# Five of eight wo products taken from the first phase of a layer kernel and made in the passage to attention

## The reference

```
x = x + mamba_and_ffn(L(x))      # state-space mixer with a scan over tokens, then a ReLU FFN 256 -> 1024 -> 256
x = x + gated(L(x))              # first use of the gated block
x = x + attention(L(x))          # 16 heads of 16
x = x + gated(L(x))              # second use, same weights

def gated(x):                    # the leading axis (8 sequences) is the step of a recurrence
    def step(c, xt):
        ft = sigmoid(xt @ wf.T + c @ uf.T + bf)
        it = sigmoid(xt @ wi.T + c @ ui.T + bi)
        gt = tanh(xt @ wc.T + c @ uc.T + bc)
        c = ft * c + it * gt
        return (c, None)
    c_final, _ = lax.scan(step, c0, x)
    return tanh(einsum('tbi,oi->tbo', x, wo) + c_final @ uo.T + bo)
```

## Time and profile before

| | us |
|---|---|
| median of 3 runs | 1632.35 |
| lowest and highest | 1628.58, 1634.82 |
| the profiled execution's own time | 1629.72 |
| its span, first to last instruction | 1627.9 |

### The profile page before, as it was taken

The page is one execution under the profiler, slowest core; times in us unless marked ns, Lnnn a source line. Parts: engine busy times, 40 slices in busy tenths (PEclk is TensorE's granted clock), DMA queues, the critical chain, the costliest instruction groups (busy, mean ns, idle before and its releaser), DMA issues.

```text
span 1627.9 us, 17393 instructions
## 1 busy us (share of the span) xinstructions
PE 1398.9 (86%) x5576; PEld 671.8 (41%) x5576; DVE 1181.1 (73%) x1836; ACT 884.7 (54%) x1513; POOL 684.1 (42%) x400
## 2 busy tenths in 40 slices
PE   6534889999999998999957999999999999989994
PEld 2202344545353545465432333434444443434442
DVE  3698898989898998860168777676868677666225
ACT  5564858585857664622212565546565655555533
POOL 2577878787879777621314122212130212100000
PEclk9866899999999999999976999999999999999997
DMA  6515161606161515100255333333232432320044
GB/s 199 174 42 192 40 221 39 222 28 221 40 207 54 193 54 181 52 26 17 62 136 117 72 80 81 91 69 77 55 91 67 92 79 50 83 53 15 15 156 142
DMA packets 93787, 158.05 MB, mean 97 GB/s; under 512 B 8592, under 2 KB 74704, under 8 KB 90576
## 3 DMA queue, kind: packets, MB, share of 16 engines
q1 hardware_dynamic: 93696, 156.94, 33.5%
HBM read 110.91 MB, written 46.01 MB: 96 GB/s over the span
## 4 chain that ended last, share of the span: by engine, by line
PE 62%; DVE 20%; issue 10%; ACT 4%; POOL 2%; DMA 2%; SPq 0%; DVEq 0%; POOLq 0%; ACTq 0%
PE psum L990 24%; PE psum L1945 8%; PE psum L1879 7%; PE psum L1853 7%; PE psum L1824 6%; PE psum L1868 5%; DVE psum L543 5%; DVE mx L1347 4%; PE psum L1035 2%; DVE middle L505 2%; DVE hb L543 1%; DVE hb L546 1%; PE psum L1819 1%; DVE stats L1323 1%; DVE bg_stats L473 1%
## 5 line engine op out<-in xcount | busy, mean ns | idle before, releaser
L1347 DVE TENSOR_REDUCE mx<-psum 128x1 f32<-128x512 f32 x512 | 344.5, 686 | 186.1 <-PE psum L1853 183.0
L1604 ACT ACTIVATE pw<-psum 128x512 f32<-128x512 f32 x512 | 301.7, 598 | 301.7 <-PE psum L1868 299.0
L920 POOL TENSOR_TENSOR hb<-ddb,bcb 128x1024 f32<-128x1024 f32 x128 | 309.7, 2442 | 65.5 <-DVE middle L505 51.6
L543 DVE TENSOR_TENSOR_SCAN psum<-psum,hb 128x512 f32<-128x512 f32 x224 | 261.5, 1213 | 29.6 <-ACT psum L736 18.1
L1853 PE MATMUL psum<-kp,qp 96*128 96x512 bf16 x512 | 208.6, 409 | 37.7 <-DVE mx L1347 27.8
L736 ACT ACTIVATE psum<-ddb,A_neg 128x512 f32<-128x512 f32 x256 | 165.3, 681 | 79.7 <-DVE hb L546 60.2
L1868 PE MATMUL psum<-qp,kp 99*128 99x512 bf16 x512 | 199.0, 390 | 8.2 <-ACT pw L1604 6.5
L1762 POOL TENSOR_TENSOR rstd<-rstd,neg_half 128x4 f32<-128x4 f32 x16 | 16.3, 1018 | 446.5 <-DVE rstd L1332 446.5
L546 DVE TENSOR_TENSOR hb<-psum,bcb 128x1024 f32<-128x1024 f32 x112 | 137.2, 1225 | 3.9
L1879 PE MATMUL psum<-pw,v_sb 128*32 128x512 f32 x1024 | 134.7, 647 | 0.5 <-ACT pw L1604 0.5
L990 PE MATMUL psum<-back,w 128*128 128x512 f32 x256 | 115.3, 605 | 8.3 <-ACT back L752 8.3
(11 more groups left out here) (200 smaller groups left out, 2203.7 us busy)
## 6 DMA issues: line engine op xcount, KB each, us to landing
ddb<-dd SPq DMA_DIRECT2D x64, 512.0 KB, 6.1
bcb<-bc SPq DMA_DIRECT2D x32, 512.0 KB, 6.5
parts<-parts_sb SPq DMA_DIRECT2D x96, 128.0 KB
dd<-dd_out SPq DMA_DIRECT2D x8, 1024.0 KB, 4.8
qp<-parts SPq DMA_DIRECT2D x32, 256.0 KB, 8.0
kp<-parts SPq DMA_DIRECT2D x16, 384.0 KB, 4.5
x_front<-x_dram SPq DMA_DIRECT2D x8, 512.0 KB, 4.0
xh<-x_front SPq DMA_DIRECT2D x8, 512.0 KB, 4.5
```

The source lines that it names most:

```text
L543: e.tensor_tensor_scan(to[:, g, :], a[:, g, :], h[:, g, :], 0.0, ALU.mult, ALU.add).then_inc(scan_ok, 1)
L920: e.tensor_tensor(hb[n % NHB], ddb[k % NSLOT][:, 1:2, :].to_broadcast([P, 2, L]), bcb[q][:, 0, :, :], ALU.mult).then_inc(bx_ok, 1)
L1347: used.up(e.tensor_reduce(mx[u % 2][:, n:n + 1], bank(used.n % 2), AXIS.X, ALU.max))
L1604: e.activation(pw[n % NPW], bank(5 + n % 2), ACT.Exp, scale=HD ** -0.5).then_inc(exp_ok, 1)
```

## The change

- `LATE = range(2, 7)`: for these five batches (gate parts of iterations 4 to 8) the first phase makes no xwo. SP stores the turned gate input X0 to `x_turned` instead of G2 to `xwo_first`, once ACT has copied it, and ACT's next write to X0 waits for this store.
- In the ring order, on PE and on ACT, z stands ahead of gi: ACT does z and its tanh at u = 4 and the input gate at u = 5. This holds for every iteration with both parts, 2 to 6.
- At the start of the second phase SP waits for the stores of `x_after_mamba` and `x_turned`, loads the five turned inputs (512 KB each) to `late_x`, and only then issues the first loads of x and xwo.
- PE makes the five products in ten pieces k of two tiles each, in banks 5, 6 and 7 by turns: k = 0, 1 behind the last xwo, k = 2 to 5 at p = -2, s = 13, and k = 6 to 9 one tile at each step s = 23 to 30 of p = -2. ACT copies each piece to one of three `late_out` buffers, which SP stores to `xwo_first`: three behind the second fetch, two at the end of p = -1.
- `late_x` and `late_out` lie where pw and ot of the second phase lie, and the first uses of these wait for the late stores.

```diff
         if gate:
             use("act", "gturn", i - 2, 2)
-            if i <= NB:
+            if i - 2 < LATE[0]:
                 use("act", "xwo", i - 2, 2)
-            use("act", "gi", i - 2, 2)
         if mid:
             use("act", "z", i + 1, 2)
+        if gate:
+            use("act", "gi", i - 2, 2)
...
-                if gate and i <= NB:
+                if gate and i - 2 < LATE[0]:
                     ring_out(e, "xwo", i - 2, 1)
                     e.dma_start(rows_of(xwo1_dram[i - 2]), tok(G2)).then_inc(xwo1_sent[(i - 2) % 2], 16)
+                if gate and i - 2 in LATE:
+                    ring_out(e, "gturn", i - 2, 1)
+                    e.dma_start(xT_dram[i - 2 - LATE[0]], feat(X0)).then_inc(xT_sent, 16)
...
             def gate_turned(b):
+                if b > LATE[0]:
+                    e.wait_ge(xT_sent, 16 * (b - LATE[0]))
...
-                    if u == 4 and gate:
-                        gate_i(i - 2)
-                    if u == 5 and mid:
+                    if u == 4 and mid:
                         mid_z(i + 1)
                         mid_tz(i + 1)
+                    if u == 5 and gate:
+                        gate_i(i - 2)
...
+            for i in range(2):
+                e.wait_ge(x1_sent[i], 16 * NB // 2)
+            e.wait_ge(xT_sent, 16 * len(LATE))
+            for n in range(len(LATE)):
+                if n == len(LATE) - 1:
+                    e.wait_ge(xr_ok, NB)
+                e.dma_start(late_x[n], xT_dram[n]).then_inc(late_in, 16)
             x_load(0)
...
+            for n in range(3):
+                late_store(n)
...
+                if p == -1:
+                    late_store(3)
+                    late_store(4)
...
+            def late_done(k):
+
+                n, u = divmod(k, 2)
+                e.wait_ge(late_pe, k + 1)
+                if n >= 3:
+                    e.wait_ge(late_sent[n - 3], 16)
+                e.activation(late_out[n % 3][:, 2 * u:2 * u + 2, :], halves(bank(5 + k % 3)), ACT.Copy).then_inc(late_act, 1)
...
+            def late_tile(k, t):
+
+                n, u = divmod(k, 2)
+                if t == 0:
+                    if k == 0:
+                        ring_out(e, "xwo", NB - 1, 1)
+                        e.wait_ge(late_in, 16 * len(LATE))
+                    if k >= 3:
+                        e.wait_ge(late_act, k - 2)
...
+                    if s == 13 and p == -2:
+                        for k in range(2, 6):
+                            late_tile(k, 0)
+                            late_tile(k, 1)
+                    if 23 <= s < 31 and p == -2:
+                        late_tile(6 + (s - 23) // 2, (s - 23) % 2)
```

More of the change, by code:

```diff
@@ L47 @@
 NSC = HU * NT
+LATE = range(2, NB - 1)
 class Count:
@@ L248, in build @@
         first.close()
+        between = ExitStack()
+        late_x = [place(between, f"late_x{i}", NF, L) for i in range(len(LATE))]
+        late_out = [place(between, f"late_out{i}", NT, D) for i in range(3)]
+        between.close()
         second = ExitStack()
@@ L293, in build @@
         x1_sent, xwo1_sent = [sem(f"x1_sent{i}") for i in range(2)], [sem(f"xwo1_sent{i}") for i in range(2)]
+        xT_sent, late_in, late_pe, late_act = sem("xT_sent"), sem("late_in"), sem("late_pe"), sem("late_act")
+        late_sent = [sem(f"late_sent{i}") for i in range(len(LATE))]
         f_var, f_rstd, h_raw, h_ok, xn_ok, xh_ok, sq_ok, m_ok = (sem(n) for n in (
@@ L757, in back_relu @@
                 ring_done(e, name, b, k)
-                if c == 6 and b > 0:
+                if c == 6 and 0 < b <= LATE[0]:
                     e.wait_ge(xwo1_sent[(b - 1) % 2], 16 * ((b - 1) // 2 + 1))
@@ L807, in act_first @@
                         gate_turned(i - 2)
-                    if u == 2 and gate and i <= NB:
+                    if u == 2 and gate and i - 2 < LATE[0]:
                         gate_xwo(i - 2)
@@ L1114, in pe_first @@
                     gate_turn(i - 2)
-                    if i <= NB:
+                    if i - 2 < LATE[0]:
                         gate_xwo(i - 2)
+                if mid:
+                    mid_in(i + 1, "z", 1)
+                if gate:
                     if i <= NB:
@@ L1368, in values_out @@
                 e.wait_ge(pv_pe, 8 * u + 4 * q + 4)
+                if q == 0 and u < 2:
+                    for n in range(len(LATE)):
+                        if n % 3 == u + 1:
+                            e.wait_ge(late_sent[n], 16)
                 if u >= 2 and q == 0:
@@ L1603, in weigh @@
                     e.wait_ge(pv_pe, (n - NPW) // 4 + 1)
+                if n == 2 * len(LATE):
+                    for k in range(0, len(LATE), 3):
+                        e.wait_ge(late_sent[k], 16)
                 e.activation(pw[n % NPW], bank(5 + n % 2), ACT.Exp, scale=HD ** -0.5).then_inc(exp_ok, 1)
@@ L1703, in act_second @@
                         cast(b + 2, 0, 0, s - 18)
+                    if s == 13 and p == -2:
+                        for k in range(2, 6):
+                            late_done(k)
                     if s == 19 and not odd and front and b + 2 > 0:
                         front_tanh(b + 2)
+                    if s in (25, 27, 29, 31) and p == -2:
+                        late_done(6 + (s - 25) // 2)
                     if s == 19 and p == -4:
@@ L1839, in pe_second @@
             token_product(ring("xwo", NB - 1, 1), 1, feat(X0), wo).then_inc(r_pe, 1)
+            def late_tile(k, t):
[6 more added lines that the diff above has]
+                        e.wait_ge(late_act, k - 2)
+                tile = slice((2 * u + t) * P, (2 * u + t + 1) * P)
+                ins = product(halves(bank(5 + k % 3))[:, t, :], [(late_x[n][:, j, tile], wo[:, j, :]) for j in range(NF)])
+                if t == 1:
+                    ins.then_inc(late_pe, 1)
+            for k in range(2):
+                late_tile(k, 0)
+                late_tile(k, 1)
             e.wait_ge(set_k, 3)
@@ L1866, in shifted @@
                 else:
-                    ring_out(e, "xwo", NB - 1, 1)
+                    e.wait_ge(late_act, 2 * len(LATE))
                 e.matmul(bank(5 + n % 2), kp[u % 3][0:NROW + 3, h, kt * P:(kt + 1) * P], qp[u % 3][0:NROW + 3, h, :],
```

19 lines of the change are left out of this document (14 added, 5 removed).

## The result

The kernel with the change takes 1635.92 us (median of 15 runs, 1632.46 to 1641.36), the kernel before beside it 1629.83 us (15 runs). The ratio is 1.0042, 95% interval 1.0031 to 1.0053: about 7 us slower, inside the forecast range of 1630 to 1656 and within the 0.5% that I called no change. The profiled execution took 1640.07 us (span 1638.3), 10.4 more than the profiled one of before, where I forecast 11.

The account below looks back on a forecast made before the run. PE runs gapless from the FFN to the forget gate, but DVE and ACT set the FFN's start in middle iterations. +11.7 - 3.5 + 2.8 = +11 on the median of 1632.35 gives 1643.3 us, range 1630 to 1656.

Parts of the forecast that it names:

- Part 1: Iterations 4 to 8 without xwo: 0 in iterations 4 to 7, -3.5 us in iteration 8.
- Part 2: z before gi, iterations 2 to 6: iterations 3 to 6 cost 2.5 us each, iteration 2 1.7, together +11.7.
- The idle piece: PE before gi's second half: some 8 us idle in iterations 4 to 6, 3.6 us in iterations 2 and 3.
- the clock loss: Low granted clock on PE's work behind the longer idle time, taken as 1.8 us per iteration.
- 0.7 for extra work behind the gate: PE has 1.72 us more work after its release at gi's second half, less 1.00 slack: 0.7 us per iteration.
- Iteration 7: No mid part; PE already waits 3.08 us for L752 before the FFN, so leaving out xwo gives 0.
- unchanged there: Expected sign: distance between FFN starts about 2.5 us longer until iteration 7, and unchanged at iteration 7.
- Part 3: Stores and waits of the first phase, with the late loads at its end: each 0.
- Part 4: Late product in the passage: -1.7 at the attention turn, +4.5 between scores 8 to 15, net +2.8 us.
- the wait for the late store: Passage, ACT's late copies wait for the first late store, meeting PE's last tile: 0 to +2 us.
- Rival A: Low clock stays away or is already paid: +2.8 to +5 first phase, 0 to +3 passage, 1632 to 1637; chance 0.22.

Follow-up runs that it names:

- e2: Kernel before with z ahead of gi in the ring, on PE and on ACT, no product moved: 1637.66 us, ratio 1.0052.
- e13: Kernel before with only batch 6's wo product moved to the passage, z ahead of gi, 3 dummy products between gi's halves: 1623.74 us, ratio 0.9966.
- e8: The change with dummy products between gi's halves, 3 in iterations 2 and 3, 8 in iterations 4 to 6: 1626.98 us, ratio 0.9979.
- e6: Kernel before with only batch 6's wo product (iteration 8's xwo) moved to the passage, gi ahead of z: 1628.88 us, ratio 0.9987.
- e3: The change with dummy products between gi's halves, 6 in iterations 2 and 3, 16 in iterations 4 to 6: 1649.86 us, ratio 1.0122.
- e9: Kernel before with four dummy matmuls behind the last xwo, ahead of the attention turn: 1630.74 us, ratio 1.0004.
- e5: The change with all ten late pieces ahead of the first score and five late_out buffers: 1634.56 us, ratio 1.0028.
- e1: The change with gi ahead of z again in the ring, on PE and on ACT: 1630.38 us, ratio 1.0006.

## Why the prediction was right, and where it was not

- **Part 1, xwo free in iterations 4 to 7, -3.5 in iteration 8: held.** e2 beside after and e13 beside e8 give 0 for iterations 4 to 6, e6 gives 3.44 for iteration 8. In iteration 7 the product is free too, but taking it out costs 0.36 (see iteration 7). In the profile of after iteration 8 gained 6.1: the other 2.7 are clock, which I had not forecast. The out product gives 1.7 (3.72 for 5.41), and goes either way behind the same wait of 2.27 us. The FFN that opens this column gives 1.0 (14.67 for 15.70). By the rule of the Trainium skill (Perfetto Trace Analysis, Identifying the Most-Contended Engine), read over the whole kernel, iteration 8 would have been free as well; the 3.44 us of e6 go against it.
- **Part 2, gi's second half behind z's first, at the low clock: the mechanism held, one size did not.** The idle piece was 7.90 us (forecast some 8), the clock loss 1.6 to 3.1 at gi (forecast 1.8). The 0.7 for extra work behind the gate did not show: e8 takes 84.30, before 84.34. DVE's shorter update (2.02 for 2.62, in e8 as in after) gives 0.6 of it back. And in iteration 6 I had not seen that the kernel before loses 1.5 itself (its out product takes 5.41 there), so the step is 0.5, not 2.5. Iterations 3 to 6 measured +6.8 for my +10. Iteration 2 measured +1.84 for my +1.7, counted from the start of its xwo (24.21 for 22.37), behind the scatter of the start.
- **Iteration 7, forecast 0: wrong, +1.25.** The failed step is "unchanged there", in two terms that I had put at nothing.
  - 0.89 is the out product's clock: 6.61 us for 5.72 behind the same wait of 6.57 us. In both kernels the chain that ended last runs through this product. e3 settles it against gi's new place in ACT's order: it has the input gate at u = 5 as well, its out product took 5.28, and its column reads 79.82, less than before. e2 (+1.0) is longer by this alone (6.76), e8 (+1.1) by this (6.43) and the next term. The length repeats with the code (5.72, 5.81 and 5.83 in before, e9 and e6; 6.61 in after and e5), so it goes with the code and not with the single execution; what sets it behind the same wait stays open.
  - 0.36 comes from the order and the missing xwo together. I had followed gi's move only where z stands ahead of it, but `gate_i` goes to u = 5 in iteration 7 too. Without xwo PE waits 2.94 us for it and the sums run at the low clock (3.64 us), so they and not ACT set the FFN's start. With xwo (e2, e13) the wait is 1.12, the sums take 1.92, and the 0.36 is absent.
- **Part 3, stores and loads 0:** nothing waits for them in the first phase's rows; e1's total agrees.
- **Part 4, the passage, +2.8: measured +2.69**, with its halves as worked out (first score 1.9 us earlier for my 1.7, from there to `nm` +4.6 for my +4.5). From the first of the eight tiles to score 15 it took 11.8 us for my 10.9, 0.7 of it the wait for the late store that I had put at 0 to 2. e5 shows the loss in the total. e9 shows that the gain at the turn alone would have been given back; in the change I cannot tell the two apart.
- **Behind `nm`, not forecast: +2.1 in the profile.** Kernels with late tiles read 751.3 to 753.6 there, those without 750.9 to 751.6. What costs this 1 us or so stays open; no run takes it apart.
- **The total.** The misses (-3.2 in iterations 3 to 6, -2.6 in iteration 8, +1.25, +2.1, and about +2 at the start, 1.8 of it scatter) cancel to within 1 us of the forecast in this one profile. That is partly luck: the profiled execution lies near the upper end of the 15 runs, and by the medians the step is 6 to 7, where I said 11. My 1643.3 also stood on a median of three runs, 1632.35, which over 15 is 1629.83. Rival A's range (1632 to 1637) held the median as well, for another reason than the one I gave: the low clock did come.

## What to carry to other kernels

When an engine has slack in a stretch, taking work from it there buys nothing, and leaving it idle can cost: price the longer idle piece by the clock of what comes behind it. Where a gap can't be closed, fill it with dummy work to its measured size and no further, and measure the size of one dummy first. Judge a stretch by its own start and end marks across several kernels, and then take out of it what one clock-dependent product adds: a column can grow by the clock of a product whose work and wait are the same as before. A total mixes a real effect with clock luck elsewhere, and a gain of clock at one place can be a loss at the next.

## What I had not expected of the hardware

- The same wait can be followed by either clock: behind 2.27 us ahead of iteration 8's out product the 16 passes took 5.41 us in before and e6, and 3.72 in after and e13. The state of such places repeats from kernel to kernel with the same code (iteration 6 of before, e6 and e9: 85.82, 85.79, 85.78).
- The mean granted clock of the whole execution was 0.930 in before and after alike, and 0.938 in e8, the only hint on the page of what the dummies win.
- One DVE instruction, the 128x1024 state update, took 1.22, 2.01 or 2.62 us by its place. POOL worked on hb through the latter two (four products in 10.30 us both times) and was idle during the first. That this is the cause was not tested, and it does not tell 2.01 from 2.62. The Trainium skill (GPSIMD Engine Reference, Key points) states that POOL shares its SBUF interfaces with VectorE, with contention for DVE instructions that have two SBUF inputs; these rows agree, as far as they go.
- Kernels with the same code up to the first mark reach it between 252.71 and 254.80 us (gi first), and between 253.72 and 255.82 (z first, with dummies). A single profile says nothing on 2 us of its total; a stretch counted from a mark close ahead of it repeated within 0.01 us (22.36 and 22.37).
